# Sums of values in two halves in both attentions, and the key-side product in the bank of the third score product

## The chip, the cores and the metric

The kernel runs on one core of a Trainium2 chip, in one launch. The metric is the device time of that launch in microseconds (us), taken as the median of several executions. The profile is one more execution, recorded by the hardware profiler. The engines are PE (TensorE, matrix products), DVE (VectorE), ACT (ScalarE), POOL (GpSimd) and SP (SyncE, which here only issues DMAs). PEld is the weight load of PE.

## The reference, cut to what matters

Two transformer layers on x of shape (8, 512, 128) with 16 heads of width 8. All inputs are float32. The first attention adds relative position terms to the scores, clipped at a distance of 64, on the query side and on the key side. The second shifts a sinusoidal relative term. The change touches the two attentions and nothing of the feed-forward parts or the norms between them.

```python
# first attention
scores = jnp.einsum('bhqd,bhkd->bhqk', Q, K) * scale
c2p = jnp.einsum('bhqd,shd->bhqs', Q, pos_key) * scale
c2p = jnp.take_along_axis(c2p, rel_pos[None, None, :, :], axis=-1)
p2c = jnp.einsum('bhkd,shd->bhks', K, pos_query) * scale
p2c = jnp.take_along_axis(p2c, p2c_pos[None, None, :, :], axis=-1)
p2c = jnp.swapaxes(p2c, -1, -2)
scores = scores + c2p + p2c
probs = jax.nn.softmax(scores, axis=-1)
ctx = jnp.einsum('bhqk,bhkd->bhqd', probs, V)
...
# second attention
scores = (term1 + term3 + _rel_shift(term2 + term4)) / jnp.sqrt(jnp.asarray(dk, dtype=x.dtype))
attn = jax.nn.softmax(scores, axis=-1)
out = jnp.einsum('bhqk,bhkd->bqhd', attn, V).reshape(B, S, H * dv)
```

## The kernel before, in words

There are five phases: tables and projections, the first attention, a mixing phase (norm, gated feed-forward, projections of the second layer), the second attention, and a dense phase. Both attentions come from `attention_phase(layer)`; `rel` is true in the first. Each runs 128 heads (8 batches by 16), one after the other, with 512 queries and 512 keys. The order on each engine is written out by hand, as one function for a step per engine: `tensor_step`, `vector_step`, `scalar_step` and `sync_step`. A step belongs to one head and has four parts, k = 0 to 3. The engines keep in order by semaphores alone. Four heads make a group (`GROUP` = 4); j % 4 is a head's place in it. The first four heads have no sums of values; the 124 others, 31 groups, have them.

Scores of 128 queries by 512 keys fill one PSUM bank. Banks 0 to 3 hold score tiles in turn. Bank 4 is `other`, banks 5 and 6 take the turned tiles, bank 7 (`cbank`) the sums of values.

A score tile (`score_tile`, L598) has two products, for the keys below and above a cut (L610, L612). In the first attention a third, small one (L616, 64 or 128 columns) goes to `other`, and DVE mixes it into the score tile by a mask (`mix`, L729). It runs score_ahead tiles ahead of the tile that is turned: 6 in the first attention, 7 in the second. Then DVE adds a band of relative terms (`finish`, L741), which a DMA has brought, and takes the row maximum (`row_max`, L749). ACT takes the exponential (`exp_tile`, L817), four tiles ahead (five in the second). Once a head's four tiles are there, PE turns them (`turn`, L631: four 128x128 float32 transposes), and ACT copies each turned tile to SBUF (`copy_turned`, L824). Called T0 to T3 and c0 to c3 below; the score tiles computed in the same step, for later heads, are s0 to s3.

The sums of values (`weigh`, L644) belong to the group before. Step j % 4 of a group does key block k = j % 4, for the four heads at once, in four column tiles of 32, each with 512 query columns. So four steps make a group's sums. They stand behind T0. ACT then copies the bank out (`group_out`, L830), at k = 1 of the group's last step, and SP stores it (`group_store`, L498) in that same step, at the end of its list.

In the first attention a head also needs a key side: a product (`key_side`, L651, 512 columns) for the head six on, behind T1, in bank 5 before the change; DVE copies it out (`key_out`, L759) behind the band add of that part. SP writes the copy to DRAM (L461) and reads it back skewed (L467), PE adds a second product into it (`correction`, L658 and L659, at the end of a step, for the head four on), ACT copies that out (L835), and SP writes it (L473) and reads it back skewed as the band (L479). The band is 512 KB; there are two band buffers. In the first attention, SP's list in step n is: key side of head n + 5 written; the band of head n + 2 read; the correction of head n + 3 written; head n + 7 loaded; key side of head n + 5 read; and in the last step of a group the store of the sums and the load of values.

The banks before the change, in the first attention: T0 in 5, T1 in 6, the key product in 5, T2 in 6, T3 in 5, the correction in 6. In the second attention T0 to T3 alternate between 5 and 6, and `edge` (L668), its own product of relative terms, is in `other`.

Of the kernel before, what the change touches and what calls it, by code (L numbers as in the profile page):

```python
# [63 lines left out]
def build(nc, t):  # L64

    top = ExitStack()
    with top:
# [267 lines left out]
        def attention_phase(layer):  # L335
# [11 lines left out]
            with ExitStack() as ctx:  # L347
# [28 lines left out]
                turned_bank = [bank[5], bank[6], bank[6], bank[5]] if rel else [bank[5], bank[6]] * 2  # L376
                key_bank, corr_bank = bank[5], bank[6] if rel else bank[4]
# [29 lines left out]
                def score_bank(h, n):  # L407

                    return score_banks[(NT * h.slot + n) % len(score_banks)]

# [126 lines left out]
                with nc.Block() as block:  # L537
# [60 lines left out]
                    def score_tile(pe, h, n):  # L598
# [14 lines left out]
                        if rel:  # L613
                            pe.wait_ge(fixed, BASE + tile)
                            a, e = fix_cols(n)
# [3 lines left out]
                    def turn(pe, h, k):  # L619
# [6 lines left out]
                        elif rel and k == 3:  # L626
                            pe.wait_ge(key_copied, BASE + made(h.n + KEY_AHEAD + 1))
                        else:
                            pe.wait_ge(copied, BASE + 4 * h.n + (k if rel else k - 1))
                        for n in range(NT):  # L630
                            last = pe.transpose(turned_bank[k][:, n * 128:(n + 1) * 128],  # L631
# [3 lines left out]
                    def weigh(pe, h, k):  # L635

                        g = h.slot // GROUP
                        if k == 0:
                            pe.wait_ge(v_in[g], BASE + 16 * (h.i + 1))
                            pe.wait_ge(out_copied, BASE + h.use(GROUP))  # L640
                            pe.wait_ge(copied, BASE + 4 * (h.n + GROUP))
                        for j in range(GROUP):
                            at = VC * (NT * j + k)
                            pe.matmul(cbank[32 * j:32 * j + VW, :], vs[g][:, at:at + VW], probt[h.slot + j][:, k, :],  # L644
                                      start=(k == 0), stop=(k == NT - 1)).then_inc(pv_mm, 1)
# [7 lines left out]
                    def correction(pe, h):  # L653

                        pe.wait_ge(sheared_in[h.slot % 4], BASE + 16 * (h.use(4) + 1))
                        for n in range(NT):
                            q = slice(128 * n, 128 * n + 128)
                            pe.matmul(corr_bank[:, q], sheared[h.slot % 4][:, q], ident[:, :], is_transpose=True, start=True, stop=False)  # L658
                            last = pe.matmul(corr_bank[:, q], stk[h.slot][:, QLO, q], tab[h.slot][:, REL:2 * REL], start=False, stop=True)  # L659
                        last.then_inc(corr_mm, 1)  # L660

                    def edge(pe, h):
# [3 lines left out]
                        for n in range(NT):  # L666
                            q = slice(128 * n, 128 * n + 128)
                            last = pe.matmul(corr_bank[:, q], stk[h.slot][:, EDGE, q], edges[:, :], start=True, stop=True)  # L668
# [6 lines left out]
                    def tensor_step(pe, i, j, left, weighed=True):  # L675
                        own = Head(i, j)
                        for k in range(NT):
                            if left >= (k + score_ahead) // NT:
                                score_tile(pe, *ahead(i, j, k, score_ahead))
                            turn(pe, own, k)  # L680
                            if k == 0 and weighed:
# [1023 lines left out]
```

## Time and profile before

| | |
|---|---|
| median of 3 runs | 2112.28 us (2108.89 to 2114.2) |
| the profiled execution: its time | 2112.18 us |
| its span, first to last instruction | 2110.4 us |
| mean clock granted to PE | 0.931 of full speed |
| busy share of PE / DVE / ACT over the span | 82% / 70% / 70% |
| first attention, turned tiles copied out | from 191.8 us on, some 760 us |
| second attention, the last of them | at 1751.8 us |

The profile's page has the busy time of each engine, the span in 40 slices, the chain that ended last and the costliest groups of instructions. A timeline row has the start in us, the duration in us, the engine, the line and operation, what is written from what, and in brackets the idle time of the engine ahead of it with what released it. Instructions on one engine overlap in part: what an instruction costs its engine is the distance to the next start, not its duration. SPq is SP's queue of DMA issues.

### The profile page before, as it was taken

The page shows a single profiled execution, that of the slowest core. Times are in us where ns is not written, and L with a number is a line of the kernel's source. Part 1 is how long each engine was busy: PE and PEld are TensorE (multiplying, and loading weights), DVE is VectorE, ACT ScalarE, POOL GpSimd, SP SyncE. Part 2 cuts the span into 40 slices and gives each one's busy share as a digit, 9 for nine tenths or more (in the row PEclk, how much of TensorE's full clock was granted, in tenths as well). Part 3 has the DMA queues.
Part 4 walks back from the last instruction along what each step waited for, and adds up shares of the span by engine and source line. Part 5 has one row for each costly group of instructions (what it writes and reads, how often), then busy time and mean ns, then how long its engine had stood idle before and what let it go on. Part 6 is the DMA issues. An engine that isn't in the chain of part 4 may idle for free. (4 is left out here: it accounts for less than half of the span.)

```text
span 2110.4 us, 44034 instructions
## 1 busy us (share of the span) xinstructions
PE 1724.6 (82%) x11670; PEld 1044.7 (50%) x11670; DVE 1468.4 (70%) x3508; ACT 1466.8 (70%) x2584; POOL 79.4 (4%) x102
## 2 busy tenths in 40 slices
PE   2316999999999999983861799999999994999998
PEld 1203555555555555552540465565556552545544
DVE  2635888888888888872983788888888882423422
ACT  2304888888888888881872799999999993223222
POOL 0000000000000000000540000000000000000000
PEclk9656999999999999996985899999999997999999
DMA  2966999998899999955687777777777763100100
GB/s 71 353 217 195 271 270 276 275 269 271 271 274 277 270 271 276 272 163 153 206 299 257 200 210 213 213 213 211 212 212 213 211 180 100 35 20 22 37 5 10
DMA packets 419996, 420.89 MB, mean 199 GB/s; under 512 B 36016, under 2 KB 325320, under 8 KB 419808
## 3 DMA queue, kind: packets, MB, share of 16 engines
q1 hardware_dynamic: 419936, 420.19, 67.1%
q8 instruction: 25, 0.41, 0.1%
q14 instruction: 35, 0.29, 0.0%
HBM read 232.47 MB, written 187.00 MB: 199 GB/s over the span
## 5 line engine op out<-in xcount | busy, mean ns | idle before, releaser
L817 ACT ACTIVATE a_prob<-bank,a_negmax 128x512 f32<-128x512 f32 x1024 | 734.6, 717 | 51.3 <-DVE a_negmax L749 49.6
L749 DVE TENSOR_REDUCE a_negmax<-bank 128x1 f32<-128x512 f32 x1024 | 699.5, 683 | 0.2 <-issue 0.2
L631 PE MATMUL bank<-a_ident,a_prob 128*128 128x128 f32 x4096 | 644.1, 280 | 60.1 <-ACT a_probt L824 50.8
L824 ACT COPY a_probt<-bank 128x512 f32<-128x512 f32 x1024 | 616.2, 602 | 87.4 <-PE bank L631 73.7
L631 PEld LDWEIGHTS bank<-a_ident,a_prob 128*128 128x128 f32 x4096 | 449.5, 141 | 181.9 <-issue 76.5
L741 DVE TENSOR_TENSOR bank<-bank,a_band 128x128 f32<-128x128 f32 (+3 forms) x1024 | 350.2, 342 | 80.1 <-PE bank L612 68.4
L610 PE MATMUL bank<-a_stks 65*128 65x192 bf16 (+7 forms) x1024 | 323.0, 316 | 10.5 <-ACT a_prob L817 10.2
L644 PE MATMUL bank<-a_probt,a_vs 128*32 128x512 f32 x2048 | 272.4, 606 | 15.0 <-ACT a_probt L824 15.0
L610 PEld LDWEIGHTS bank<-a_stks 65*128 65x128 bf16 (+1 forms) x1024 | 100.1, 98 | 231.8 <-ACT a_prob L817 202.4
L729 DVE COPY_PREDICATED bank<-a_mask,bank 128x128 f32<-128x128 uint32 (+1 forms) x512 | 139.4, 272 | 107.2 <-PE bank L616 107.1
L612 PE MATMUL bank<-a_stks 65*128 65x320 bf16 (+5 forms) x768 | 201.1, 262 | 0.0
L1586 DVE TENSOR_TENSOR d_drop<-bank,d_s 128x128 f32<-128x128 f32 x32 | 7.1, 284 | 170.4 <-PE bank L1509 170.4
L835 ACT COPY a_corr<-bank 128x512 f32<-128x512 f32 x128 | 76.3, 596 | 66.9 <-PE bank L659 66.9
L616 PE MATMUL bank<-a_stks 65*128 65x128 bf16 (+1 forms) x512 | 110.7, 216 | 12.4 <-DVE bank L729 2.9
L658 PE MATMUL bank<-a_ident,a_sheared 128*128 128x128 f32 x512 | 106.4, 285 | 14.4 <-DMA a_sheared<-shear_a 14.2
L1488 PE MATMUL bank<-d_ha,d_h1T 128*128 128x512 f32 x256 | 112.3, 592 | 0.0
L1488 PE MATMUL bank<-d_hb,d_h2T 128*128 128x512 f32 x256 | 111.2, 592 | 0.0
L759 DVE COPY a_keyside<-bank 128x512 f32<-128x512 f32 x128 | 87.3, 682 | 28.6 <-DMA a_mask<-in_mask 13.1
L754 DVE COPY a_corr<-bank 128x512 f32<-128x512 f32 x128 | 87.2, 682 | 17.2 <-PE bank L668 9.9
L659 PE MATMUL bank<-a_tabs,a_stks 65*128 65x128 bf16 x512 | 97.5, 224 | 0.0
L668 PE MATMUL bank<-edges,a_stks 96*128 96x128 bf16 x512 | 51.0, 223 | 51.3 <-DMA a_ident<-in_ident 43.8
L651 PE MATMUL bank<-a_stks,a_tabs 65*128 65x512 bf16 x128 | 50.5, 395 | 49.5 <-DMA a_mask<-in_mask 47.5
(169 smaller groups left out, 1567.9 us busy)
## 6 DMA issues: line engine op xcount, KB each, us to landing
a_band<-shear_b SPq DMA_DIRECT2D x128, 512.0 KB, 4.4
shear_a<-a_keyside SPq DMA_DIRECT2D x128, 256.0 KB, 3.4
a_sheared<-shear_a SPq DMA_DIRECT2D x128, 256.0 KB, 4.4
shear_b<-a_corr SPq DMA_DIRECT2D x128, 256.0 KB, 4.4
shear_e<-a_corr SPq DMA_DIRECT2D x128, 256.0 KB, 2.3
a_band<-shear_e SPq DMA_DIRECT2D x128, 256.0 KB, 3.4
a_stks<-stack SPq DMA_DIRECT2D x128, 192.0 KB, 4.5
a_stks<-stack SPq DMA_DIRECT2D x128, 144.0 KB, 2.9
```

Source lines behind the costliest of these rows:

```text
L610: last = pe.matmul(score[:, 0:c], k[:, qlo, q], k[:, klo, 0:c], start=True, stop=True)
L612: last = pe.matmul(score[:, c:T], k[:, qhi, q], k[:, khi, c:T], start=True, stop=True)
L616: last = pe.matmul(other[:, 0:e - a], k[:, qhi, q], k[:, khi, a:e], start=True, stop=True)
L631: last = pe.transpose(turned_bank[k][:, n * 128:(n + 1) * 128], prob[h.slot % 2][:, n, k * 128:(k + 1) * 128], ident[:, :])
L644: pe.matmul(cbank[32 * j:32 * j + VW, :], vs[g][:, at:at + VW], probt[h.slot + j][:, k, :], start=(k == 0), stop=(k == NT - 1)).then_inc(p ...
L658: pe.matmul(corr_bank[:, q], sheared[h.slot % 4][:, q], ident[:, :], is_transpose=True, start=True, stop=False)
L729: v.copy_predicated(score[:, a:e], mask[:, 0:e - a], other[:, 0:e - a]).then_inc(fixed, 1)
L741: v.tensor_tensor(score[:, a:e], score[:, a:e], band[h.slot % bands][:, n, w:w + e - a], ALU.add).then_inc(added, 1)
L749: v.tensor_reduce(negmax[h.slot % 2][:, n:n + 1], score[:, :], AX.X, ALU.max, negate=True).then_inc(maxed, 1)
L817: nc.scalar.activation(prob[h.slot % 2][:, n, :], score[:, :], ACT.Exp, bias=negmax[h.slot % 2][:, n:n + 1]).then_inc(exped, 1)
L824: nc.scalar.copy(probt[h.slot][:, k, :], turned_bank[k][:, :]).then_inc(copied, 1)
L1488: last = pe.matmul(dst[:, :], w[:, k, 128 * m:128 * m + 128], src[:, k, :], start=(k == 0), stop=(k == KH - 1))
```

## The change

Four things are changed; SP's program is not.

1. In both attentions `weigh` does key blocks 1 to 3 in two pieces of 256 query columns: the first behind T0, as before, the second behind T2. Key block 0 stays in one piece.
2. `group_out` moves from k = 1 to k = 3 of the group's last step.
3. In the first attention banks 5 and 6 alternate over T0, T1, T2, T3 and the correction, from head to head. A turn waits for the copy of what was two turns before it in that bank.
4. In the first attention the key product goes to `other`. PE waits for the mix of s1 ahead of it, and the third product of s2 waits until DVE has copied the key product out. DVE copies it out ahead of the band add and no longer behind it.

```diff
@@ banks @@
-                turned_bank = [bank[5], bank[6], bank[6], bank[5]] if rel else [bank[5], bank[6]] * 2
-                key_bank, corr_bank = bank[5], bank[6] if rel else bank[4]
+                swing = bank[5:7]
+                key_bank = other
...
+                def turned_bank(h, k):
+
+                    return swing[(h.slot + k) % 2] if rel else swing[k % 2]
+
+                def corr_bank(h):
+
+                    return swing[h.slot % 2] if rel else other
@@ score_tile, the third product @@
-                    def score_tile(pe, h, n):
+                    def score_tile(pe, h, n, keys_out=None):
...
                             pe.wait_ge(fixed, BASE + tile)
+                            if keys_out is not None:
+                                pe.wait_ge(key_copied, BASE + keys_out)
@@ turn @@
                             pe.wait_ge(corr_copied, BASE + made(h.n + corr_ahead))
-                        elif rel and k == 3:
-                            pe.wait_ge(key_copied, BASE + made(h.n + KEY_AHEAD + 1))
+                        elif rel:
+                            pe.wait_ge(copied, BASE + 4 * h.n + max(k - 1, 0))
                         else:
-                            pe.wait_ge(copied, BASE + 4 * h.n + (k if rel else k - 1))
+                            pe.wait_ge(copied, BASE + 4 * h.n + k - 1)
@@ weigh @@
-                    def weigh(pe, h, k):
+                    def weigh(pe, h, k, half):
...
+                        q = slice(0, T) if k == 0 else slice(half * T // 2, half * T // 2 + T // 2)
                         for j in range(GROUP):
                             at = VC * (NT * j + k)
-                            pe.matmul(cbank[32 * j:32 * j + VW, :], vs[g][:, at:at + VW], probt[h.slot + j][:, k, :],
-                                      start=(k == 0), stop=(k == NT - 1)).then_inc(pv_mm, 1)
+                            part = pe.matmul(cbank[32 * j:32 * j + VW, q], vs[g][:, at:at + VW], probt[h.slot + j][:, k, q],
+                                             start=(k == 0), stop=(k == NT - 1 and half == 1))
+                            if k == 0 or half == 1:
+                                part.then_inc(pv_mm, 1)
@@ tensor_step @@
-                                score_tile(pe, *ahead(i, j, k, score_ahead))
+                                score_tile(pe, *ahead(i, j, k, score_ahead), made(own.n + KEY_AHEAD + 1) if rel and k == 2 else None)
                             turn(pe, own, k)
-                            if k == 0 and weighed:
-                                weigh(pe, Head(i, j - j % GROUP - GROUP), j % GROUP)
+                            if weighed and (k == 0 or k == 2 and j % GROUP > 0):
+                                weigh(pe, Head(i, j - j % GROUP - GROUP), j % GROUP, k // 2)
...
                             if rel and k == 1 and left >= KEY_AHEAD:
-                                pe.wait_ge(copied, BASE + 4 * own.n + 1)
+                                pe.wait_ge(fixed, BASE + 4 * own.n + 1 + score_ahead + 1)
                                 key_side(pe, Head(i, j + KEY_AHEAD))
@@ vector_step @@
+                                if rel and k == 1 and left >= KEY_AHEAD:
+                                    key_out(v, Head(i, j + KEY_AHEAD))
                                 if rel and left >= (k + score_ahead) // NT:
                                     finish(v, *ahead(i, j, k, score_ahead))
                                 if not rel and k == 3 and left >= corr_ahead:
                                     edge_out(v, Head(i, j + corr_ahead))
-                                if rel and k == 1 and left >= KEY_AHEAD:
-                                    key_out(v, Head(i, j + KEY_AHEAD))
@@ scalar_step @@
                                 copy_turned(act, own, k)
-                                if k == 1 and weighed and j % GROUP == GROUP - 1:
+                                if k == 3 and weighed and j % GROUP == GROUP - 1:
                                     group_out(act, Head(i, j - j % GROUP - GROUP))
```

## Rows read from the trace of the kernel before

**Rows 1.** The page, its first line.
```profile
span 2110.4 us, 44034 instructions
```
**Rows 2.** Windows in the two attentions: busy PE, PEld, DVE, ACT, POOL; clock, DMA.
```profile
500.00:600.00 100.00, 93.39 (x743) 57.98 (x741) 85.30 (x220) 87.04 (x157) 0.00 (x0) 1.00 0.90 272
1400.00:1500.00 100.00, 94.49 (x788) 60.52 (x785) 88.91 (x204) 98.38 (x185) 0.00 (x0) 1.00 0.76 212
```
**Rows 3.** Timeline of one step of the first attention, PE: start, duration.
```profile
506.07 0.63 PE L631 MATMUL bank<-a_ident,a_prob 128*128 128x128 f32 x4 [0.18 <-ACT a_probt L824]
506.62 1.07 PE L644 MATMUL bank<-a_probt,a_vs 128*32 128x512 f32 x8
...
507.62 0.39 PE L610 MATMUL bank<-a_stks 65*128 65x512 bf16 x1
507.85 0.19 PE L616 MATMUL bank<-a_stks 65*128 65x64 bf16 x1
507.88 0.63 PE L631 MATMUL bank<-a_ident,a_prob 128*128 128x128 f32 x4
508.35 0.38 PE L651 MATMUL bank<-a_stks,a_tabs 65*128 65x512 bf16 x1
508.57 0.24 PE L610 MATMUL bank<-a_stks 65*128 65x192 bf16 x1
...
509.19 0.66 PE L631 MATMUL bank<-a_ident,a_prob 128*128 128x128 f32 x4 [0.18 <-ACT a_probt L824]
509.68 0.30 PE L610 MATMUL bank<-a_stks 65*128 65x320 bf16 x1
...
510.22 0.65 PE L631 MATMUL bank<-a_ident,a_prob 128*128 128x128 f32 x4
...
511.40 0.35 PE L610 MATMUL bank<-a_stks 65*128 65x448 bf16 x1
...
512.01 0.63 PE L631 MATMUL bank<-a_ident,a_prob 128*128 128x128 f32 x4 [0.18 <-ACT a_probt L824]
```
**Rows 4.** Timeline of the same step, DVE.
```profile
508.19 0.23 DVE L729 COPY_PREDICATED bank<-a_mask,bank 128x64 f32<-128x64 uint32 x1 [0.91 <-PE bank L616]
508.33 0.69 DVE L749 TENSOR_REDUCE a_negmax<-bank 128x1 f32<-128x512 f32 x1
508.93 0.36 DVE L741 TENSOR_TENSOR bank<-bank,a_band 128x192 f32<-128x192 f32 x1
509.20 0.68 DVE L759 COPY a_keyside<-bank 128x512 f32<-128x512 f32 x1
509.79 0.28 DVE L729 COPY_PREDICATED bank<-a_mask,bank 128x128 f32<-128x128 uint32 x1
509.99 0.68 DVE L749 TENSOR_REDUCE a_negmax<-bank 128x1 f32<-128x512 f32 x1
```
**Rows 5.** Timeline of the same step, ACT: the last exponential and the last copy.
```profile
510.71 0.69 ACT L817 ACTIVATE a_prob<-bank,a_negmax 128x512 f32<-128x512 f32 x1 [0.24 <-DVE a_negmax L749]
511.29 0.58 ACT L824 COPY a_probt<-bank 128x512 f32<-128x512 f32 x1
```
**Rows 6.** Timeline about the end of a group, ACT, SP's queue and DVE.
```profile
520.92 0.59 ACT L830 COPY a_outs<-bank 128x512 f32<-128x512 f32 x1
...
521.76 0.38 SPq L498 DMA_DIRECT2D heads_out<-a_outs  x1
...
523.48 0.32 SPq L479 DMA_DIRECT2D a_band<-shear_b  x1
...
529.00 0.37 DVE L741 TENSOR_TENSOR bank<-bank,a_band 128x192 f32<-128x192 f32 x1 [0.49 <-DMA a_band<-shear_b]
```
**Rows 7.** The line of the band's read (L479), all 128: time to landing.
```profile
DMA to landing us min/median/max: 3.4/4.4/6.4
```
**Rows 8.** Timeline in the second attention, first step of a group, PE and ACT.
```profile
1411.99 1.06 PE L644 MATMUL bank<-a_probt,a_vs 128*32 128x512 f32 x8 [0.41 <-ACT a_probt L824]
...
1413.86 0.58 ACT L824 COPY a_probt<-bank 128x512 f32<-128x512 f32 x1 [0.27 <-PE bank L631]
```

More of the change, by code:

```diff
@@ L625, in turn @@
                             pe.wait_ge(corr_copied, BASE + made(h.n + corr_ahead))
-                        elif rel and k == 3:
-                            pe.wait_ge(key_copied, BASE + made(h.n + KEY_AHEAD + 1))
+                        elif rel:
+                            pe.wait_ge(copied, BASE + 4 * h.n + max(k - 1, 0))
                         else:
-                            pe.wait_ge(copied, BASE + 4 * h.n + (k if rel else k - 1))
+                            pe.wait_ge(copied, BASE + 4 * h.n + k - 1)
                         for n in range(NT):
-                            last = pe.transpose(turned_bank[k][:, n * 128:(n + 1) * 128],
+                            last = pe.transpose(turned_bank(h, k)[:, n * 128:(n + 1) * 128],
                                                 prob[h.slot % 2][:, n, k * 128:(k + 1) * 128], ident[:, :])
                         last.then_inc(turned, 1)
-                    def weigh(pe, h, k):
+                    def weigh(pe, h, k, half):
                         g = h.slot // GROUP
@@ L657, in correction @@
                             q = slice(128 * n, 128 * n + 128)
-                            pe.matmul(corr_bank[:, q], sheared[h.slot % 4][:, q], ident[:, :], is_transpose=True, start=True, stop=False)
-                            last = pe.matmul(corr_bank[:, q], stk[h.slot][:, QLO, q], tab[h.slot][:, REL:2 * REL], start=False, stop=True)
+                            pe.matmul(corr_bank(h)[:, q], sheared[h.slot % 4][:, q], ident[:, :], is_transpose=True, start=True, stop=False)
+                            last = pe.matmul(corr_bank(h)[:, q], stk[h.slot][:, QLO, q], tab[h.slot][:, REL:2 * REL], start=False, stop=True)
                         last.then_inc(corr_mm, 1)
@@ L667, in edge @@
                             q = slice(128 * n, 128 * n + 128)
-                            last = pe.matmul(corr_bank[:, q], stk[h.slot][:, EDGE, q], edges[:, :], start=True, stop=True)
+                            last = pe.matmul(corr_bank(h)[:, q], stk[h.slot][:, EDGE, q], edges[:, :], start=True, stop=True)
                         last.then_inc(corr_mm, 1)
@@ L719, in _ @@
                         for k in range(NT):
-                            weigh(pe, Head(loops, FIRST + last - GROUP), k)
+                            for half in range(2 if k else 1):
+                                weigh(pe, Head(loops, FIRST + last - GROUP), k, half)
                     def mix(v, h, n):
@@ L753, in edge_out @@
                         v.wait_ge(e_written[h.slot % 2], BASE + 16 * h.use(2))
-                        v.tensor_copy(corr[h.slot % 2][:, :, :], corr_bank[:, :].rearrange("p (n r) -> p n r", n=NT)).then_inc(corr_copied, 1)
+                        v.tensor_copy(corr[h.slot % 2][:, :, :], corr_bank(h)[:, :].rearrange("p (n r) -> p n r", n=NT)).then_inc(corr_copied, 1)
                     def key_out(v, h):
@@ L823, in copy_turned @@
                             act.wait_ge(pv_mm, BASE + 16 * (h.use(GROUP) - vslots + 1))
-                        nc.scalar.copy(probt[h.slot][:, k, :], turned_bank[k][:, :]).then_inc(copied, 1)
+                        nc.scalar.copy(probt[h.slot][:, k, :], turned_bank(h, k)[:, :]).then_inc(copied, 1)
                     def group_out(act, h):
@@ L834, in corr_out @@
                         act.wait_ge(b_written, BASE + 16 * (h.n - 1))
-                        nc.scalar.copy(corr[h.slot % 2][:, :, :], corr_bank[:, :].rearrange("p (n r) -> p n r", n=NT)).then_inc(corr_copied, 1)
+                        nc.scalar.copy(corr[h.slot % 2][:, :, :], corr_bank(h)[:, :].rearrange("p (n r) -> p n r", n=NT)).then_inc(corr_copied, 1)
                     @block.scalar
```

## Prediction, made before the changed kernel had run

> **What bounds the kernel now.** The chip runs one core. The page's slices show two long flat stretches, the two attentions; the windows view of one piece of each [rows 2] says what fills them. In the first, TensorE (PE), VectorE (DVE) and ScalarE (ACT) are each 85 to 93% busy and none is full, so a loop of waits between engines sets the time. In the second ACT is 98.4% busy: it is the bound. The clock column reads 1.00, full speed, in both.
>
> For the loop I read the timeline of one head, engine by engine [rows 3 to 5]. One step turns four tiles of a head (T0 to T3, L631), each copied out by ACT (c0 to c3, L824), and between them computes four score tiles of later heads (s0 to s3, L610 to L616). T0 starts at 506.07 and the next T0 at 512.01: a step is 5.94 us. What releases what, each term a difference of two starts: T0 to the value sums (weigh, L644) 0.55; their own time 1.00; s1 to its mix on DVE (L729) 0.57; mix to row maximum 0.14, to band add 0.60, to key copy (L759) 0.27, to next mix 0.59, to row maximum 0.20; to the exponential exp3 0.72, to c3 0.58, to the next T0 0.72 (the ACT copy is named as releaser). The sum is 5.94, the whole step: this chain is the bound, and DVE's 0.91 of idle ahead of the mix is its visible mark. PE itself idles about 0.9 in a step, so that is all a shorter chain could bring.
>
> **The change, first attention.** Times below count from T0 of a step. Weighing in halves applies in three steps of four: j = 0 of a group still weighs in one piece.
>
> Half the sums go behind T2. A 512-column bf16 product lets the next start 0.22 later (508.35 to 508.57 [rows 3]). If the four float32 sums, side by side, need four times that, 0.88 of their 1.00 is columns and 0.12 is fixed; a half then costs 0.44 + 0.12 = 0.56. Bounds for a half: 0.50 (all scales) and 0.65. Ahead of the sums PE takes 0.55 after a turn, where a score tile follows one after 0.49 (509.19 to 509.68); a second piece pays that second gap too, 0.06, or nothing at the low end.
> The Trainium skill, TensorEngine Tiling (Array Packing), Key Properties, says that a change of tiling mode drains the engine. The sums use 128x32 tiles between 128x128 ones, so by it the fixed part is paid at each piece, which speaks against the change; without it a half would be 0.50 and a step 0.18 shorter than by my sum. The longer gap agrees with it; no row shows a half.
>
> The alternating banks take away T2's wait for c1 (the [0.18 <-ACT] at 509.19). But the key product moves to the bank of the third score product. It must wait until DVE has read that bank (the mix), and s2's third product must wait until DVE has copied the key side out. Before, PE never waited for that round. Costs: mix 0.23 and 0.07 to PE (the gap of 510.07, end of a mix, to the work behind it, T3 at 510.22, is 0.15, of which the third product takes about 0.08), key product 0.38, 0.15 until DVE can start (third product ends 508.04, mix 508.19): the key copy starts 0.83 after the mix, against 0.74 if DVE alone decided. It lasts 0.68, and T2 follows 0.15 after its end. The bounds of this round are 0.09 less and, if every crossing costs 0.05 more, 0.15 more.
>
> Step with halves: weigh 0.55, s1 1.11, mix 1.68, key copy 2.51, T2 3.34, second half 3.89, s3 4.45, T3 0.28 later (s1 to T1 is 0.26, with 64 fewer columns) 4.73; from T3 to the next s0 it is 1.18 (510.22 to 511.40: turn and correction), so 5.91, and T0 at 6.19. The other chain, over mix at T2 + 0.31, row maximum, exp3, c3, gives c3 at 5.15; T3 gives it at 5.34 (a copy starts about 0.61 after its turn: 1.87 from weigh to c1, less 1.00 and 0.26 [rows 8]), and 5.34 + 0.72 = 6.06 is earlier than 6.19. So PE itself now sets the step: 6.19, **0.25 longer**. It gives up 0.84 waiting for the key copy and gains 0.44 from the earlier s1; the other half of the sums is only moved. Bounds: 6.01 and 6.52.
>
> Step j = 0, whole sums: s1 1.55, mix 2.12, key copy 2.95, T2 3.78, mix 4.09, row maximum 4.29, exp3 5.01, c3 5.59, T0 6.31, 0.37 longer.
>
> Then the copy of the sums (group_out, L830) moves from k = 1 to k = 3 of the group's last step. On ACT it costs what it did, as the same copy takes another place in the list. Behind it stand the head's correction copy and, through out_copied, two others: PE's next weigh, 0.55 behind T0 and so still covered, and **SP's queue**, which isn't changed. SP stores the group (L498) in that step and issues nothing until the copy is there. Now the copy starts at 520.92, the store issues 0.84 later and the band read of the head after next (L479) 1.72 after the store [rows 6]; in the profile this read already lands late once a group (DVE waits 0.49 at 529.00). After the change the copy starts near c3 + 0.5, that is 0.35 ahead of the next T0; the store issues 0.5 behind it, the band read 2.2. Landing takes 4.4 in the median, 3.4 at least [rows 7], 5.5 here: the band is there at 6.6 (5.6 to 7.7), and DVE wants it at row maximum + 0.60 = 4.89. DVE then finishes, mixes 0.30 later, and T0 follows that mix by 0.43 (509.79 to 510.22): 7.33 in place of 6.31, **1.02 more** for each group (0.02 to 2.1). The other reads behind it have about a head of lead more, and I put them at nothing; if that cover is gone, each costs as much again.
>
> Group of four: 3 x 0.25 + 0.37 + 1.02 = 2.14. There are 31 groups with sums: 31 x 2.14 = **66 us** more (18 with every term low, 135 with every term high, the round 0.15 longer in j = 0 too).
>
> **Second attention.** Its key product and banks stay. ACT can give back at most its idle 1.6% [rows 2], over 31 groups of some 17.9 us 9 us. That idle comes once a group, where weigh waits for the last copy (0.41) and c1 then waits for T1 (0.27) [rows 8]. This stays: now weigh waits for the sums' copy instead, queued right behind the last one. In the other steps s1 comes 0.44 earlier, which helps, but PE's work grows by 0.06 + 0.12, and PE is 94.5% busy, about 0.23 free in a head. I take **5 us** less, between 9 less and 10 more.
>
> The start, the mixing and the dense stages aren't touched. The profiled execution took 2112.18 us, its span 2110.4 [rows 1], and the median is 2112.28; no correction is needed. Forecast: 2112.2 + 66 - 5 = **2173 us**.
>
> **Rivals.** (B) The band read is in time: SP's late store drains the queue, and the read lands in 3.4 or DVE is late anyway. The row of 0.49 waited in the old order speaks against it, the emptier queue for it. Then 3 x 0.25 + 0.37 = 1.12 a group, 35 us, less 5: 2142; with the low half and gap 2121.
> (C) Faster. The pieces of the sums overlap with their neighbours, so that a turn with half the sums behind it takes 0.75 and not 1.11, and the key copy follows the row maximum at once. The chain over exp3 is then 0.55 + 0.50 + 0.57 + 1.88 (mix to mix) + 0.20 + 0.72 + 0.58 + 0.72 = 5.72, and PE's own path 5.7 to 5.8: 0.2 under today. With j = 0 at 6.22 a group gains 0.3, 10 us, the second attention 9: 2093. It decides as soon as the step with halves is under 5.82, so that three of them pay for j = 0. For it speaks that 1.00 of sums sits on today's chain; against it, the 0.55 gap and DVE's row maximum ahead of the key copy, which no bank removes.
> (D) The pieces cost their low ends and the band is in time, with a bit of overlap: within 0.3%, 2106 to 2118.
>
> **Numbers.** A difference under 0.3%, about 6 us, can't be told from no change. Chances: forecast 0.50, B 0.24, C 0.16, D 0.10. Hence slower 0.74, same 0.10, faster 0.16. The range reaches down over B to D's middle, 2112, and up to 2212, where the band costs nearly all of its bound; that leaves C and a thin top.
>
> **What would show it.** In a step with halves: T0 to T0 near 6.2; two rows of L644 of about 0.6 each; s2's third product (L616) waiting 0.8 for DVE L759; DVE idle ahead of both mixes; T2 no longer released by ACT. At each j = 0: DVE L741 waiting over 1 us for the band, SP waiting long for ACT L830, a step of 7.3. In the second attention, ACT still 98% busy and a group near 17.7. If the L741 wait stays as it is, B is right; if T0 to T0 is under 5.9, my price of the round or of the halves is wrong. The forecast fails too if PE's semaphores cost more on the key round, as it is crossed three times a step.

## The result and the profile after

The changed kernel takes 2244.16 us (median of 4 runs) against 2113.23 us for the kernel before: a ratio of 1.062, 95% interval 1.057 to 1.067. It is 131 us slower, where 61 were forecast. Its profiled execution has a span of 2250.2 us, 139.8 over that of before [rows 1].

Where the time went, by the first and the last copy of a turned tile (L824, after the change L838) in each attention, start to start: the first took 758.5 us and takes 887.3, **128.8 more**; the second took 573.4 and takes 583.9, **10.5 more**. What lies between and behind them is unchanged within 2 us.

The page after, the span and the slices (busy tenths of PE, then the granted clock in tenths of full speed):

```profile
span 2250.2 us, 47232 instructions
...
PE   2407888888888888888386189999999996899998
...
PEclk9657999899999988999698589999999998899999
```

Before, PE was at 9 in the whole first attention and the clock at full speed; now both flicker. One group of four heads mostly costs 23.7 or 23.8 us before; after, of the 28 full groups (heads 8 to 119) 11 take 26.1 to 26.5 us at a clock of 1.00, and 17 take 27.7 to 31.0 us at a mean clock of 0.94 to 0.83; for most of the attention the two kinds alternate. Two neighbours, windows from one copy of the sums to the next (busy PE, PEld, DVE, ACT, POOL, then the clock, the DMA share and GB/s):

```profile
522.42:550.93 28.51, 23.52 (x202) 14.19 (x201) 21.56 (x54) 21.29 (x39) 0.00 (x0) 0.94 0.79 227
550.93:577.42 26.49, 22.28 (x202) 13.65 (x201) 21.52 (x53) 21.06 (x38) 0.00 (x0) 1.00 0.84 245
```

The short kind is 2% over what the prediction summed, 4 x 5.94 + 2.14 = 25.9. The long kind has a part of its time at a lower clock, which the prediction didn't have at all.

PE in a step with halves, T0 to T0 (to be read beside [rows 3]):

```profile
516.56 0.61 PE L641 MATMUL bank<-a_ident,a_prob 128*128 128x128 f32 x4
517.10 0.64 PE L655 MATMUL bank<-a_probt,a_vs 128*32 128x256 f32 x8
517.67 0.39 PE L618 MATMUL bank<-a_stks 65*128 65x512 bf16 x1
...
517.92 0.63 PE L641 MATMUL bank<-a_ident,a_prob 128*128 128x128 f32 x4
518.56 0.39 PE L664 MATMUL bank<-a_stks,a_tabs 65*128 65x512 bf16 x1
...
519.84 0.23 PE L626 MATMUL bank<-a_stks 65*128 65x128 bf16 x1 [0.67 <-DVE a_keyside L773]
519.91 0.61 PE L641 MATMUL bank<-a_ident,a_prob 128*128 128x128 f32 x4
520.44 0.64 PE L655 MATMUL bank<-a_probt,a_vs 128*32 128x256 f32 x8
521.01 0.31 PE L618 MATMUL bank<-a_stks 65*128 65x320 bf16 x1
...
521.30 0.61 PE L641 MATMUL bank<-a_ident,a_prob 128*128 128x128 f32 x4
...
522.70 0.61 PE L641 MATMUL bank<-a_ident,a_prob 128*128 128x128 f32 x4
```

The rows show a step of 6.14 us (6.19 in the sum), each half taking 0.57 behind a gap of 0.53 or 0.54 (0.56 and 0.55), and the third product waiting for DVE's key copy.

The next step is the first of a group, j = 0, whose band read stands behind the late store. ACT, SP's queue and DVE (to be read beside [rows 6]):

```profile
522.42 0.59 ACT L844 COPY a_outs<-bank 128x512 f32<-128x512 f32 x1
...
523.26 0.38 SPq L506 DMA_DIRECT2D heads_out<-a_outs  x1
...
524.98 0.32 SPq L487 DMA_DIRECT2D a_band<-shear_b  x1
...
530.39 0.37 DVE L755 TENSOR_TENSOR bank<-bank,a_band 128x192 f32<-128x192 f32 x1 [2.75 <-DMA a_band<-shear_b]
```

T0 was at 522.70, so the store issues 0.56 and the read 2.28 behind it (0.5 and 2.2 in the sum), and it lands after 5.4, not 4.4. The step from this T0 to the next, at 531.25, takes 8.55 us, where the sum had 7.33. In the next group, a short one, the same three rows:

```profile
551.78 0.38 SPq L506 DMA_DIRECT2D heads_out<-a_outs  x1
...
554.08 0.32 SPq L487 DMA_DIRECT2D a_band<-shear_b  x1
...
558.44 0.37 DVE L755 TENSOR_TENSOR bank<-bank,a_band 128x192 f32<-128x192 f32 x1 [2.12 <-DMA a_band<-shear_b]
```

Here the read issues 2.30 behind the store in place of 1.72, and lands after 4.3; the step takes 8.05. Both kinds alternate in this way through the attention, and in the kernel before too: SP's loop is eight heads long, so it holds two groups, and in only one of the two does the read come close behind the store.

Back to the first of the two groups, PE in the timeline and in windows of one us (stretch, length, busy PE, clock, DMA share, GB/s):

```profile
528.74 0.19 PE L620 MATMUL bank<-a_stks 65*128 65x64 bf16 x1
531.06 0.23 PE L626 MATMUL bank<-a_stks 65*128 65x128 bf16 x1 [2.12 <-DVE bank L743]
531.25 0.95 PE L641 MATMUL bank<-a_ident,a_prob 128*128 128x128 f32 x4
532.13 1.08 PE L655 MATMUL bank<-a_probt,a_vs 128*32 128x256 f32 x8
```

```profile
530.00:531.00 1.00, 0.00 (x0) 1.00 1.10 246
531.00:532.00 1.00, 0.94 (x5) 0.70 0.99 266
532.00:533.00 1.00, 1.00 (x9) 0.50 0.91 174
533.00:534.00 1.00, 1.00 (x8) 0.50 0.90 258
534.00:535.00 1.00, 1.00 (x7) 0.59 1.03 348
535.00:536.00 1.00, 0.33 (x4) 1.00 1.17 357
```

PE stood idle for 2.12 us for the band, and then worked at half clock, 1.2 GHz, for some 3.4 us: a half of the sums takes 1.08 by its row in place of 0.64. The step from 531.25 to the next T0 at 538.80 took 7.55 us in place of 6.14.

So the late band costs the first step of a group, and the clock the steps behind it. The mean length of both over the 28 full groups, from the starts of T0 in the rows of L631 (L641 after the change):

| | first step of a group, us | its other three steps, us |
|---|---|---|
| before | 6.01 | 17.81 |
| the sum of the prediction | 7.33 | 18.57 |
| changed, 11 groups at clock 1.00 | 7.87 | 18.45 |
| changed, 5 groups at 0.94 | 8.21 | 19.90 |
| changed, 4 groups at 0.88 or 0.89 | 8.45 | 21.05 |
| changed, 8 groups at 0.83 | 8.28 | 22.46 |

### The profile page after: what moved, and what is told of

The parts are those of the page before. It is cut to its first block and busy times, and to the rows that moved or that the text cites. A ratio compares the mean times of both kernels' runs of the same rounds, so it can differ in the third digit from the quotient of the medians.

```text
span 2250.2 us, 47232 instructions
## 1 busy us (share of the span) xinstructions
PE 1786.8 (79%) x13206; PEld 1074.0 (48%) x13206; DVE 1500.9 (67%) x3508; ACT 1488.5 (66%) x2584; POOL 79.8 (4%) x102
## 5 line engine op out<-in xcount | busy, mean ns | idle before, releaser
L831 ACT ACTIVATE a_prob<-bank,a_negmax 128x512 f32<-128x512 f32 x1024 | 725.0, 708 | 83.7 <-DVE a_negmax L763 78.2
L838 ACT COPY a_probt<-bank 128x512 f32<-128x512 f32 x1024 | 610.6, 597 | 156.6 <-PE bank L641 148.6
L641 PE MATMUL bank<-a_ident,a_prob 128*128 128x128 f32 x4096 | 656.8, 285 | 5.4 <-ACT a_probt L838 3.1
L641 PEld LDWEIGHTS bank<-a_ident,a_prob 128*128 128x128 f32 x4096 | 465.2, 146 | 85.8 <-issue 41.7
L655 PE MATMUL bank<-a_probt,a_vs 128*32 128x256 f32 (+1 forms) x3584 | 323.1, 436 | 33.6 <-ACT a_outs L844 33.2
L618 PE MATMUL bank<-a_stks 65*128 65x192 bf16 (+7 forms) x1024 | 333.1, 325 | 2.5 <-ACT a_prob L831 2.3
L620 PE MATMUL bank<-a_stks 65*128 65x320 bf16 (+5 forms) x768 | 205.8, 268 | 0.0
L626 PEld LDWEIGHTS bank<-a_stks 65*128 65x128 bf16 x512 | 51.1, 100 | 194.4 <-DVE a_keyside L773 105.7
L655 PEld LDWEIGHTS bank<-a_probt,a_vs 128*32 128x32 f32 x3584 | 74.0, 110 | 115.0 <-issue 76.0
L671 PE MATMUL bank<-a_ident,a_sheared 128*128 128x128 f32 x512 | 111.8, 296 | 14.6 <-DMA a_sheared<-shear_a 13.5
L773 DVE COPY a_keyside<-bank 128x512 f32<-128x512 f32 x128 | 88.5, 691 | 42.1 <-PE bank L664 26.5
```

The costliest lines, as they stand in the source:

```text
L618: last = pe.matmul(score[:, 0:c], k[:, qlo, q], k[:, klo, 0:c], start=True, stop=True)
L620: last = pe.matmul(score[:, c:T], k[:, qhi, q], k[:, khi, c:T], start=True, stop=True)
L626: last = pe.matmul(other[:, 0:e - a], k[:, qhi, q], k[:, khi, a:e], start=True, stop=True)
L641: last = pe.transpose(turned_bank(h, k)[:, n * 128:(n + 1) * 128], prob[h.slot % 2][:, n, k * 128:(k + 1) * 128], ident[:, :])
L655: part = pe.matmul(cbank[32 * j:32 * j + VW, q], vs[g][:, at:at + VW], probt[h.slot + j][:, k, q], start=(k == 0), stop=(k == NT - 1 and h ...
L671: pe.matmul(corr_bank(h)[:, q], sheared[h.slot % 4][:, q], ident[:, :], is_transpose=True, start=True, stop=False)
```

## The experiments

Three parts of the forecast could be at fault: the key product's round (steps), the block of SP's queue (groups), and something that the sum left out. The theory from the changed kernel's profile: steps as forecast, the block dearer than forecast, and the clock behind it a cost of its own. The rival: the halves cost more than they free. The first four kernels separate the parts. Times are medians; ratios are to the kernel before.

### SP's store one step later, all else as changed

```diff
 # sync_step, first attention only
                         if left > 2:
                             shear_b_write(sp, Head(i, j + 3))
+                        if weighed and store_now and j % GROUP == 0:
+                            group_store(sp, Head(i, j - 2 * GROUP), left + 1 >= GROUP * (vslots - 1))
...
-                    if weighed and j % GROUP == GROUP - 1:
+                    if not rel and weighed and j % GROUP == GROUP - 1:
```

> The changed kernel, but in the first attention SP stores a group's sums (and loads the next values) one step later, behind that step's band read and correction write, so that nothing that the scores need stands behind the late copy of the sums. Theory (the late copy blocks SP's queue): the waits of DVE's band add for the band go from 59 us in the window 300 to 1000 to under 10, the granted clock there comes back to 1.00, a group takes 3 x 6.15 + 6.3 = 24.8 us, the first attention 31 x 1.0 = 30 to 35 us more than before, the second stays 11 us longer: 2155 us. Rival (the band waits come from DMAs slowed by something else, the bank change or the halves): the waits stay and the time stays over 2200.

Measured: 2162.2 us, ratio 1.023 (1.021 to 1.025). No row of the waits from 300 to 900 us names the band any more, against 27 waits and 50.9 us in the changed kernel. Groups take 24.8 and 24.9 us, as forecast: 6.36 for the first step and 18.48 for the other three. The first attention takes 785.0, 27 more than before, a little under the 30 to 35 expected. The window from 300 to 900 us:

```profile
300.00:900.00 600.00, 531.08 (x4836) 327.64 (x4834) 520.06 (x1256) 508.79 (x895) 0.00 (x0) 1.00 0.85 261
```

The clock column reads 1.00 again. So one move in SP's list takes away 102 of the first attention's 129 us. Against the table above, over 28 groups, 49 us of it are first steps and 49 us the other three. The second attention, which the theory had unchanged, takes 602.8 here, 19 more than in the changed kernel: every third group there takes 19.7 to 22.2 us in place of 18.3, with a pause of SP at the loop's border (no issue from 1281.23 to 1284.93). This kernel's SP program is longer (one round of the loop is written out); that this is the reason was not tried, but the kernel below whose program has the old length (and whole sums in the second attention) doesn't show it.

### The banks alone

The changed kernel with `weigh` whole and the copy of the sums at k = 1, as before; the banks, the waits and DVE's order as changed.

```diff
 # to the changed kernel
-                            if weighed and (k == 0 or k == 2 and j % GROUP > 0):
-                                weigh(pe, Head(i, j - j % GROUP - GROUP), j % GROUP, k // 2)
+                            if k == 0 and weighed:
+                                weigh(pe, Head(i, j - j % GROUP - GROUP), j % GROUP)
...
-                                if k == 3 and weighed and j % GROUP == GROUP - 1:
+                                if k == 1 and weighed and j % GROUP == GROUP - 1:
```

> The kernel before with only the banks of the first attention changed: key product in the bank of the third score product, banks 5 and 6 alternating. Sums of values whole, copy of the sums at k = 1. Theory (the round PE, DVE, PE of the key product lengthens each step): every step takes 6.3 us in place of 5.94, so 128 x 0.37 = 47 us more: 2159 us, no band wait beyond those of before, second attention unchanged. Rival (the freed turns pay for the round): within 10 us of before.

Measured: 2156.49 us, ratio 1.020 (1.018 to 1.022). Groups take 25.3 and 25.4 us, 6.34 a step (6.31 in the sum), the second attention 573.7. The first attention takes 803.4, 45 more than before; with the first experiment's 785.0 beside it, the halves give back 18 of that. One row carries the 45, PE's third product of s2:

```profile
504.04 0.23 PE L626 MATMUL bank<-a_stks 65*128 65x128 bf16 x1 [0.68 <-DVE a_keyside L769]
```

### The copy of the sums late, alone

```diff
-                                if k == 1 and weighed and j % GROUP == GROUP - 1:
+                                if k == 3 and weighed and j % GROUP == GROUP - 1:
```

> The kernel before with one edit: the copy of the sums at k = 3 of the group's last step and no longer at k = 1. Theory (SP's queue stands behind it): each of 31 groups loses 2 to 3 us to the band, 60 to 95 us in the first attention: 2190 us, DVE's band add waiting over 2 us once a group. The second attention moves by under 3 us, as SP is not held there. Rival (the block costs only the 1.02 us a group of my sum): 2144 us. Rival (halves cause it): no change.

Measured: 2219.43 us, ratio 1.052 (1.048 to 1.056). One digit, on an engine that isn't full, costs 107 us, 29 more than the theory's 78, which had no term for the clock either; the first attention takes 866.5 us, the second 572.6, as before. So neither halves nor banks are needed for it. Of 28 full groups two took 25.1 and 25.6 us at a clock of 1.00, the rest 26.8 to 30.2 at 0.94 or 0.83. The first step is 8.29 us in the mean, 2.28 over before, the other three 19.33, 1.52 over before. The end of one wait, PE, and the clock in windows behind it:

```profile
515.39 0.23 PE L616 MATMUL bank<-a_stks 65*128 65x128 bf16 x1 [2.40 <-DVE bank L729]
```

```profile
515.00:516.00 1.00, 0.61 (x3) 0.81 0.96 275
516.00:517.00 1.00, 1.00 (x8) 0.50 0.68 176
517.00:518.00 1.00, 1.00 (x8) 0.50 0.91 201
518.00:519.00 1.00, 1.00 (x7) 0.50 0.91 301
519.00:520.00 1.00, 1.00 (x10) 0.98 1.11 385
```

### The copy at k = 2, alone

```diff
-                                if k == 1 and weighed and j % GROUP == GROUP - 1:
+                                if k == (2 if rel else 1) and weighed and j % GROUP == GROUP - 1:
```

> The kernel before with the copy of the sums at k = 2 in the first attention, one part of a step earlier than in the kernel that had it at k = 3 alone (2219 us). The block of SP's queue is some 1.3 us shorter. Theory (two costs, the band wait itself and, once PE has idled some 2 us, its clock at half): the wait falls from 2.5 to about 1.2 us a group, the clock stays at 1.00, the first attention takes 25 to 35 us more than before: 2142 us. Rival (only the wait counts, in proportion): 107 x 1.2 / 2.5 = 50 us more, 2163.

Measured: 2137.88 us, ratio 1.013 (1.011 to 1.015); the first attention 779.3 us, 21 more than before (25 to 35 expected), groups 24.0 to 25.7, the clock 1.00. One part of a step less of block takes away 87 of the 108 us. That isn't a cost in proportion to the wait, the rival's 50 us: from 300 to 900 us DVE waits 29.8 us for the band, half of the 60.7 with the copy at k = 3, and the cost is a fifth. The clock isn't all of that, as a part of every wait is covered: at k = 3 the first wait of a group is 2.83 us in the mean and its step is only 2.28 longer. The next experiment takes the clock apart from the wait.

### The late copy, with PE kept busy

```diff
-                    def score_tile(pe, h, n):
+                    def score_tile(pe, h, n, again=0):
...
+                        for _ in range(again):
+                            pe.matmul(score[:, 0:c], k[:, qlo, q], k[:, klo, 0:c], start=True, stop=True)
                         if rel:
                             pe.wait_ge(fixed, BASE + tile)
...
-                                score_tile(pe, *ahead(i, j, k, score_ahead))
+                                score_tile(pe, *ahead(i, j, k, score_ahead), 9 if rel and weighed and k == 0 and j % GROUP == 1 else 0)
```

> The kernel with only the copy of the sums late (2219 us), and nine repeats of one score product (448 columns, 0.19 us each) where PE would stand idle for the late band, in the second step of each group. The result is the same, PE has 1.7 us more to do per group. Theory (the clock is a cost of its own, paid after PE has idled over 2 us): the idle stretch shrinks to some 0.7 us, the granted clock stays at 1.00 in all groups, a group takes 25 to 26 us in place of 27 to 30 with the same waits for the band, 2166 to 2185 us: more work, less time. Rival (the band wait alone makes the time): 2219 us or a little more.

Measured: 2185.6 us, ratio 1.034 (1.031 to 1.038): 34 us less than without the extra work, just over the upper end of what was expected; the clock didn't stay at 1.00 in all groups, as 6 of the 28 took 27.8 to 28.4 us at 0.94, behind idles of PE of 1.1 to 1.6 us, less than the theory's two. The late copy alone first, then with PE kept busy, each the window 300 to 900 us and its row of waits for the band:

```profile
300.00:900.00 600.00, 519.62 (x3851) 313.67 (x3851) 444.56 (x1141) 457.66 (x810) 0.00 (x0) 0.93 0.79 236
...
DVE bank L741 <- DMA a_band<-shear_b: 60.7, 23, 3.8
```

```profile
300.00:900.00 600.00, 552.53 (x4219) 334.88 (x4219) 463.67 (x1188) 476.12 (x845) 0.00 (x0) 0.99 0.83 246
...
DVE bank L743 <- DMA a_band<-shear_b: 65.1, 29, 3.4
```

DVE waits for the band as long as before, yet the clock is up from 0.93 to 0.99 and the time is down. The steps say where: the first step of a group is 8.29 us in the mean in both kernels, and the other three fall from 19.33 to 18.13 (17.81 before), 34 us over 28 groups. The clock is thus a cost of its own. Six groups still pay it, so 34 is a lower bound of it in this kernel; by the steps it is up to 43.

### The key copy made short

```diff
-                        v.tensor_copy(keyside[h.slot % 2][:, :], key_bank[:, :]).then_inc(key_copied, 1)
+                        w = T if isinstance(h.n, int) and h.n < KEY_AHEAD else 64
+                        v.tensor_copy(keyside[h.slot % 2][:, 0:w], key_bank[:, 0:w]).then_inc(key_copied, 1)
```

> The kernel with the banks alone changed (2156 us), but DVE copies only 64 of the 512 columns of each key product out (the rest of the key side is left as it was, so the scores' key-side terms are left out but for those columns). Theory (the round mix, key product, key copy, third product sets the step): the copy takes 0.2 in place of 0.68 us, the step falls from 6.34 to the 5.85 to 5.95 of the next chain, 2156 - 55 = 2100 us. Rival (the turns' new bank order costs): 2156 us.

Measured: 2109.69 us, ratio 0.999 (0.998 to 1.000), 47 us less than with the whole copy. The same third product waits 0.16 to 0.21 for the copy and no longer 0.68. The rest of the way to 2100 went to the band: 22.5 us of waits in 33 places, against one wait of 0.5 with the whole copy. So the round is what the banks cost. What the new order of banks 5 and 6 gives or costs by itself isn't shown: the short copy also takes some 0.5 us out of DVE's part of every step, and the chain of before [rows 4] went through that copy too.

### Halves with the old banks

First the halves in both attentions (the change's `weigh` and its calls), the copy at k = 3 and SP's store one step later, as above; nothing of the banks:

> The kernel before with the sums in halves in both attentions and the copy of the sums at k = 3, but the banks as before and SP's store one step later in the first attention. Theory: on the old chain the half gives back 0.44 us in three steps of four (5.50), j = 0 stays at 5.94: 31 x 1.32 = 41 us less in the first attention, 11 more in the second as in the changed kernel: 2082 us. The DMA engines are 91% busy before, so at 5.6 us a head they would be at 0.96; if they bound it, 2095. Rival (a half costs as much as it frees, as PE's own work is the bound): the same as before, 2112 to 2123.

Measured: 2122.73 us, ratio 1.005 (1.004 to 1.006). The time lies in the rival's range, but not for the rival's reason: the first attention takes 745.9 us, 13 less than before, though not 41; the second takes 601.1, 28 more, with the pause of SP that the first experiment had too. Then the halves in the first attention only, SP's loop shifted so that its program is no longer than before:

```diff
+                            second = 2 if rel else None
+                            split = second is not None and j % GROUP > 0
+                            if weighed and (k == 0 or split and k == second):
+                                weigh(pe, Head(i, j - j % GROUP - GROUP), j % GROUP, (0 if k == 0 else 1) if split else None)
...
+                        start = 2 * GROUP if rel else FIRST
+                        turns = (NHEAD - start - load_ahead) // unroll
...
+                        with sp.Fori(0, turns) as i:
+                            for j in range(unroll):
+                                sync_step(sp, i, start + j, NHEAD, store_now=True)
```

> The kernel before with halves in the first attention only, the copy of the sums at k = 3 there and SP's store one step later (SP's loop begins at step 8, so its program is no longer than before); the second attention as before. Theory: the first attention as in the kernel with halves in both and the store one step later, 12 us less than before, the second 573: 2100 us. Rival (SP's displaced store costs elsewhere too): 2112.

Measured: **2100.69 us, ratio 0.995 (0.994 to 0.996)**: faster than both kernels. The first attention takes 747.1, 11 less than before, the second 574.2. And the store alone:

> The kernel before with only SP's store (and load of values) one step later in the first attention. Theory: the gain of the kernel with halves and this store is that of the halves; alone the store takes away the band waits of before, 9 us in 18 places, most of them after a group: 2106 to 2112 us. Rival (the store makes the whole gain): 2100 us.

Measured: 2109.24 us, ratio 0.9986 (0.9975 to 0.9997), so it is not the store that makes the gain. Why 11 and not 41, by smaller loads (`head_load`) in the faster kernel:

```diff
-                        sp.dma_start(stk[j][0:SR, :, :], stack[0][b, own].rearrange("c j a t -> (c j) a t")).then_inc(stk_in[j], 16)
+                        sp.dma_start(stk[j][0:8, :, :], stack[0][b, own].rearrange("c j a t -> (c j) a t")[0:8]).then_inc(stk_in[j], 16)
```

> The kernel with halves in the first attention and SP's store one step later (2101 us), but each head's load brings 8 rows of 48, 32 KB in place of 192 KB; 40 rows of the head's stack are left out, so its scores lack those terms. It takes a tenth of the first attention's bytes away. Theory (that kernel's gain of 12 us in place of the 41 of my sum is cut by the DMA engines, which are 92% busy: the band comes late 55 times in 600 us): the waits for the band fall from 47 to under 15 us, a group takes 22.5 to 22.8 in place of 23.5, 2070 to 2080 us. Rival (the engines' own chain gives no more): 2101 us.

Measured: 2078.06 us, ratio 0.984 (0.981 to 0.986). Most groups take 22.7 us, and the first attention 729.1, 18 less. The waits for the band fall less far than expected (under 15). The rows of waits for the band from 300 to 900 us, with the whole load and with the small one:

```profile
DVE bank L753 <- DMA a_band<-shear_b: 47.0, 55, 1.7
```

```profile
DVE bank L753 <- DMA a_band<-shear_b: 18.3, 30, 1.9
```

The DMA share goes from 0.92 to 0.83. What the halves freed on PE's chain was met by the DMA engines: a group can be 1.1 us shorter (22.7 against 23.8), and with the whole loads some 0.35 of that is left. The sum's 1.32 a group isn't there even then: in the groups of 22.7 us a step with halves takes 5.60 in the mean, not 5.50. So of the 41 us, 11 came, 18 more came with the smaller loads, and most of the rest is a half's gain priced too high, 0.34 a step and not 0.44.

### Halves in the second attention

The first attention as before, `second = None if rel else 2` in the lines above and the copy at k = 3 in the second only:

> The kernel before with the halves, and the late copy of the sums, in the second attention only. Theory (T3 comes later by the second half ahead of it, and the exponential of the head two on waits for T3, as it overwrites that head's tiles): a group takes 18.3 in place of 17.97 us, the second attention 11 us more, the first unchanged: 2123 us. Rival (the 11 us were the late copy or a slow clock left over by the first attention): 2112.

Measured: 2124.12 us, ratio 1.006 (1.005 to 1.008), the second attention 583.9 us, groups of 18.3. The 11 us are the halves' own. In the changed kernel's timeline, PE's T3 and ACT behind it:

```profile
1515.36 0.60 PE L641 MATMUL bank<-a_ident,a_prob 128*128 128x128 f32 x4
```

```profile
1515.26 0.63 ACT L838 COPY a_probt<-bank 128x512 f32<-128x512 f32 x1
1516.00 0.69 ACT L831 ACTIVATE a_prob<-bank,a_negmax 128x512 f32<-128x512 f32 x1
```

T3 ends at 1515.96 and the exponential starts 0.04 later. It starts 0.74 behind the start of the copy ahead of it, where the others of this stretch start 0.46 to 0.48 behind theirs, so it is some 0.27 late: `exp_tile` waits for the turns of the head two before (`turned`), whose tiles it overwrites.

Then the same with `second = None if rel else 3`:

> As the one with halves in the second attention only, but the second half stands behind T3, not behind T2. The same instructions. Theory (T3 ahead of the half is what counts): T3 comes 0.6 us earlier, the exponential doesn't wait, a group takes 17.7 us, the second attention 7 us less than before: 2105 us. Rival (PE's own added work, 0.25 a head, is the bound): the same 18.3 as behind T2, 2123 us.

Measured: 2111.56 us, ratio 1.000 (0.999 to 1.001), groups of 17.9 and 18.0, the second attention 571.5. Moving the same instructions behind T3 gives back 12.4 us, so it is the place of the half that costs. The 7 us of gain on top didn't come, only 2: half of the theory fell. What is left of ACT's idle is what was there before: once a group weigh waits for the copy of the sums and c1 for T1. One such place, PE and ACT:

```profile
1516.48 1.06 PE L645 MATMUL bank<-a_probt,a_vs 128*32 128x512 f32 x8 [0.71 <-ACT a_outs L835]
...
1518.35 0.59 ACT L829 COPY a_probt<-bank 128x512 f32<-128x512 f32 x1 [0.34 <-PE bank L631]
```

## Why the prediction was wrong

The direction was right, and so were the two mechanisms that the sum had, the key round and the late band; a step was within 1%. A third mechanism, the clock, was not in it, and the band's term was too small. The sum was half of the truth. By its own steps, over the 28 full groups: the steps and halves 29 us measured (31 in the sum), the late band 49 (29), the clock 49 (nothing).

- **The key round.** Step with halves 6.19 forecast, 6.14 measured; whole sums 6.31 and 6.34. The third product waits 0.67, where the sum had 0.84 from where PE could first have gone on. Right; the short key copy shows that it is this round.
- **A half.** 0.56 forecast, 0.57 measured, and its gap of 0.54. The rule of the Trainium skill (TensorEngine Tiling (Array Packing), Key Properties) that each change of tiling mode drains the engine was put up against plain scaling (0.50); the rows agree with it, as two halves take 1.14 where the whole takes 1.00. That the drain is what makes the difference isn't shown by them.
- **SP's queue: a term mis-sized.** The sum had 1.02 us a group; the first step is 1.50 longer than 6.36 in the groups at full clock, and 1.76 in the mean of all. It put together rows that don't belong together. The issue times came from one group [rows 6], the landing, 4.4, was the median of all reads [rows 7]. In groups of that kind the read issued on time and landed after 4.8 to 5.5 us; the row of before that showed this, 5.5, stood in the prediction and was used for the bound only. In the groups of the other kind it landed after 4.0 to 4.3, but issued 0.57 later. DVE waited 2.1 to 2.9 us in the first kind and 1.8 to 2.1 in the second, 1.7 in the sum. A read that always issues behind the same transfers should be priced by the rows in that place, for every group of the loop. That it "already lands late once a group" was also read from one group: of before's groups every second one has that wait.
- **The clock: the step that failed.** "The clock column reads 1.00, full speed, in both" was read as a property of the kernel and never asked again, though the prediction itself had PE idle for the band once a group. In the 17 groups that ran in part at half clock the three steps behind the first take 19.8 to 22.6 us, and 18.5 in the 11 others, which is also what they take with SP's store moved. That is 49 of the 129 us. The late copy alone shows the same with no other change, 43 us of it, and 34 us came back when PE was given idle work. The prediction had no term for it, and its upper bound, 2212, was therefore too low.
- **Rival B** (the band in time) and **C** (faster) were wrong here. But C's ground, that the halves shorten the chain if nothing else is done, holds: with the old banks and the store moved the kernel is 0.5% faster.
- **The second attention.** 5 us less forecast, 10.5 more measured, just outside its own bounds (9 less to 10 more). The sum looked at weigh and c1 only. It missed that T3 releases an exponential: PE's time up to T3 grew by the extra gap and fixed part, and T3 had no slack. The added PE work was named, and its cover, PE's 5.5% of idle, was an average, not slack at T3.

Of the whole difference, then: the block and the clock behind it 102 us (first experiment), the round and the halves together 27, the second attention 10.5. They add up to 139 and not to 131, as they are read in the profiled execution, which took 2251.94 us, 8 over the median.

## What to carry to other kernels

A copy moved later on an engine with slack still holds every queue that waits for it: list what is behind that wait in the DMA issuer's program, and move the store behind the reads that the next work needs. Price a stall of TensorE twice, once for the wait and once for the work behind it at half clock; here stalls of 1.1 to 4.2 us were followed by half clock, though not each of them. And a term taken off the critical chain of one engine is worth only what the next resource leaves: here, with the DMA engines 92% busy, 11 of at least 29 us.

## What the runs showed of the hardware that I had not expected

- The clock fell after a single stall in a stream that had run at full speed: PE idle from 528.9 to 531.06, half clock until about 534.8. After 2.40 us of idle (late copy alone, up to 515.39) it was at half for some 3.4 us too; in the groups of 0.88 and 0.83 it stayed there longer.
- The length of the stall alone didn't tell whether it fell. In the late copy alone an idle of 1.93 us left it at full speed (1.00 from 490 to 491 us), and one of 1.62 did so with the copy at k = 2. In the changed kernel 1.17 us of idle was followed by half clock (0.53 from 446 to 447 us). The rows of PE, in this order:

```profile
489.26 0.23 PE L616 MATMUL bank<-a_stks 65*128 65x128 bf16 x1 [1.93 <-DVE bank L729]
```

```profile
907.17 0.23 PE L616 MATMUL bank<-a_stks 65*128 65x128 bf16 x1 [1.62 <-DVE bank L729]
```

```profile
445.75 0.23 PE L626 MATMUL bank<-a_stks 65*128 65x128 bf16 x1 [1.17 <-DVE bank L743]
```

- With the copy at k = 2 the clock never fell from 300 to 900 us.
- More work made a kernel faster: nine more score products in each group, and 34 us less.
- The cost of a late copy is steep: at k = 1 nothing, at k = 2 26 us, at k = 3 107 us.
- The same 512 KB read of the band landed after 4.8 to 5.5 us when it was issued 1.7 us behind the store, and after 4.0 to 4.3 when it was issued 2.3 behind it (changed kernel, full groups). That the distance is the cause was not tried.
